# The expert stage in two phases, with the last four attention blocks routed inside the first

## The reference

```
probs = sigmoid(h @ router_w.T)                  # 8 experts
topw, sel = top_k(probs, 2); topw /= topw.sum(-1) + 1e-20
y = square(relu(h @ W1[e])) @ W2[e]              # widths 4 x 256, 4 x 512
out = x + gb * sum over the 2 chosen of topw * y
```

## Time and profile before

| | |
|---|---|
| median of 3 runs | 2789.18 us |
| profiled execution, first to last instruction | 2796.0 us |
| up to the end of attend | 2145.6 us |
| dispatch_rest and the start of experts, to the transposes of tile 1 | 112.0 us |
| from there to the last matmul of tile 38 | 470.0 us |
| last adds and gate_out | 68.4 us |

### The profile page before, as it was taken

One profiled execution on the slowest core, in us unless ns is written; L12 is line 12 of the kernel. 1 busy time (PEld: TensorE's weight loads), 2 busy tenths in 40 slices (PEclk: granted clock), 3 DMA queues, 4 the chain that ended last, 5 costly groups with the idle time before them and its releaser, 6 DMA issues. The chain is left out here.

```text
span 2796.0 us, 49392 instructions
## 1 busy us (share of the span) xinstructions
PE 2529.9 (90%) x16192; PEld 1298.9 (46%) x16192; DVE 2179.1 (78%) x5287; ACT 1727.6 (62%) x3481; POOL 692.7 (25%) x721
## 2 busy tenths in 40 slices
PE   7978999999999999999999999999996579999990
PEld 6852333333333333333333333333332479999990
DVE  6979889888888788888888898888821867777761
ACT  4640576777666666666666667666674257777760
POOL 3453333000010101011010110101012435556553
PEclk9986899999999999999999999999998689999995
DMA  6989788412404234040431404234012635555548
GB/s 213 316 280 301 275 282 286 145 27 57 97 28 97 56 73 116 13 117 29 96 92 37 120 22 104 52 78 105 16 54 84 217 84 92 88 90 91 91 68 255
DMA packets 218336, 331.82 MB, mean 119 GB/s; under 512 B 27408, under 2 KB 158224, under 8 KB 218096
## 3 DMA queue, kind: packets, MB, share of 16 engines
q1 hardware_dynamic: 137728, 170.48, 21.4%
q0 software_dynamic: 58704, 136.86, 19.7%
q10 hardware_dynamic: 21664, 21.50, 2.5%
HBM read 140.75 MB, written 187.20 MB: 117 GB/s over the span
## 5 line engine op out<-in xcount | busy, mean ns | idle before, releaser
L1007 ACT ACTIVATE probs<-ps 128x512 f32<-128x512 f32 (+3 forms) x2400 | 1122.2, 539 | 587.5 <-PE ps L1335 339.4
L1033 DVE TENSOR_REDUCE early<-ps 128x1 f32<-128x512 f32 x1536 | 1001.5, 684 | 106.0 <-PE ps L1240 100.1
L1240 PE MATMUL ps<-kh,qs 96*128 96x512 bf16 (+3 forms) x2560 | 882.2, 361 | 88.0 <-DVE early L1033 37.4
L1335 PE MATMUL ps<-qs,kh 99*128 99x512 bf16 (+3 forms) x2560 | 831.1, 352 | 17.0 <-ACT probs L1007 6.6
L1351 PE MATMUL ps<-probs,vs 128*32 128x512 f32 (+3 forms) x5120 | 605.8, 545 | 0.0
L1240 PEld LDWEIGHTS ps<-kh,qs 96*128 96x128 bf16 x2560 | 250.7, 99 | 700.5 <-DVE early L1033 303.6
L1029 DVE CUSTOM_DVE_ANT_0 junk<-ps,causal 128x128 bf16<-128x128 f32 (+3 forms) x1024 | 480.7, 483 | 52.8 <-PE ps L1240 48.0
L1335 PEld LDWEIGHTS ps<-qs,kh 99*128 99x128 bf16 x2560 | 246.1, 98 | 290.7 <-ACT probs L1007 135.8
L1760 POOL DMA_INDIRECT acc<-y,to x156 | 250.6, 1606 | 119.0 <-ACT y L1815 73.9
L926 POOL DMA_INDIRECT rows_out<-row,place_a x96 | 95.2, 991 | 698.5 <-DVE place_a L697 650.8
L1339 PE MATMUL ps<-ident_b,causal_b 128*128 128x128 bf16 x1024 | 214.0, 221 | 0.0
(11 more groups left out here) (231 smaller groups left out, 3011.2 us busy)
## 6 DMA issues: line engine op xcount, KB each, us to landing
rows_out<-row POOLq DMA_DIRECT2D x129, 544.0 KB, 3.6
xg<-rows_out SPq DMA_DIRECT2D x39, 544.0 KB
v_ones<-vt SPq DMA_DIRECT2D x16, 1024.0 KB, 6.4
vs<-v_ones SPq DMA_DIRECT2D x16, 1024.0 KB, 11.2
contexts<-ctx_out SPq DMA_DIRECT2D x64, 256.0 KB
q_parts<-parts SPq DMA_DIRECT2D x32, 384.0 KB, 4.6
k_parts<-parts SPq DMA_DIRECT2D x32, 384.0 KB, 4.6
qs<-q_parts SPq DMA_DIRECT2D x64, 192.0 KB, 7.3
```

The lines of the kernel that those rows point to most:

```text
L1007: nc.scalar.activation(probs[u % PB][:, h, q0:TB], bank(s % SB)[:, q0:TB], ACT.Exp, scale=SCALE).then_inc(exp_done, 1)
L1033: nc.vector.tensor_reduce(early[:, h, t, k0 // CW:k0 // CW + 1], tile, AX.X, ALU.max).then_inc(max_done, 1)
L1240: nc.tensor.matmul(tile[:, 0:w], qh[a % HR][0:STACK, t * P:(t + 1) * P], kh[a % HR][0:STACK, k0:k0 + w], start=True, stop=True).then_inc(m ...
L1335: mm = nc.tensor.matmul(tile[:, q0:TB], kh[a % HR][:, kt * P:(kt + 1) * P], qh[a % HR][:, j * TB + q0:(j + 1) * TB], start=True, stop=not ...
```

## The change

The table of tiles is made in two parts. After the 12 blocks of attend, at least FULL = 17 full tiles exist whatever the routing is. These are listed at once (`first_table`, 22 small DVE steps) and run first. The four late blocks are finished inside the steps of these tiles, at fixed steps: block m begins at step 1 + 12m, so one block takes part in three tiles. Then the table of the LATE = 22 tiles is made (`late_need`, `late_table`, `tile_rows` at steps 59 to 61), and these run as before. 17 + 22 is again 39. Other parts:

- w1 is loaded whole in attend (3.1 MB). w2 is loaded whole (3.1 MB) at the start of experts and split once into w2_hi and w2_lo: ACT makes four high parts of 1536 columns, DVE two low parts and POOL two; PE waits for all before its loop. The split per tile (L1797, L1872) is gone.
- Since w2 stays in place, `down` reads it at an address from a register, and PE computes that address by an instruction ahead of each of the 12 matmuls. Tiles of width 256 read a neighbour's slices, and relu's scale `wide` (0 or 1) zeroes the upper half.
- `down` adds up in the same two banks for every tile, and so waits in its first step for the `weigh` of the tile before. `tails` moves from POOL to DVE.
- The gate of attention is folded into wo_g once; square is in place.

```diff
+FULL = -(-(2 * HIDDEN_BLOCKS * TB - E * (TB - 1)) // TB)
+LATE = (2 * T - FULL * TB + E * (TB - 1)) // TB
+STEP_LAG = 2
+PITCH = 12
+BASE = [1 + PITCH * m for m in range(LATE_BLOCKS)]
+SECOND_TABLE = BASE[-1] + L_PUT + 1
+SEND_FROM = [(b + L_PUT + 1) // FW - 1 for b in BASE[:-1]] + [(BASE[-1] + L_PUT) // FW - 2]
+SENDS = [3] * (LATE_BLOCKS - 1) + [8]
...
+                def gather(i):
+                    if i == FULL:
+                        sp.wait_ge(table_steps, BOTH_TABLES)
+                        for p in range(2):
+                            sp.wait_ge(sent[p], 64 * LATE_BLOCKS)
...
+                for n in range(SPLITS // 2, SPLITS):
+                    own = slice(n * piece, (n + 1) * piece)
+                    pool.wait_ge(w2h_done, n + 1)
+                    nc.gpsimd.tensor_tensor(w2_lo[:, own, :], w2_lo[:, own, :].bitcast(F32),
+                                            w2_hi[:, own, :].bitcast(F32), ALU.subtract).then_inc(w2lp_done, 1)
...
+                def send(m, part):
+                    if part == 0:
+                        pool.wait_ge(placed, m + 1)
+                        pool.wait_ge(tails_set, 3 + m + 1)
...
+                for i in range(NT):
+                    add(i)
+                    for m in range(LATE_BLOCKS):
+                        done = SENDS[m] * (i - SEND_FROM[m])
+                        if 0 <= done < 2 * TT:
+                            for part in range(done, min(done + SENDS[m], 2 * TT)):
+                                send(m, part)
...
+                def tails(i):
+                    dve.reg_load(kind, tiles[0:1, i, 3:4])
+                    e = dve.snap(kind, min_val=0, max_val=E - 1)
+                    dve.wait_ge(xg_in[i % 2], 16 * (i // 2 + 1))
+                    if i >= 3:
+                        dve.wait_ge(y_done, TT * (i - 2))
+                        dve.wait_ge(added, 16 * TT * (i - 2))
...
                     if f == 1 and i + 1 < NT:
                         low_rows(i + 1)
+                        tails(i + 1)
+                    for m in range(LATE_BLOCKS):
+                        late(m, q - STEP_LAG - BASE[m])
+                    if q == SECOND_TABLE + STEP_LAG + 2:
+                        tile_rows(41, LATE, FULL)
...
                 def down(q):
                     i, f = divmod(q, FW)
-                    p = i % 2
+                    if f == 0:
+                        pe.reg_load(slab, tiles[0:1, i, 1:2])
+                        at["slice"] = pe.snap(slab, min_val=0, max_val=NW - FW)
                     pe.wait_ge(lo_done, q + 1)
                     for t in range(TT):
-                        o = bank(2 + 2 * p + t // 2)[:, (t % 2) * D:(t % 2 + 1) * D]
+                        if f == 0 and i and t % 2 == 0:
+                            pe.wait_ge(y_done, TT * (i - 1) + t + 2)
+                        o = bank(2 + t // 2)[:, (t % 2) * D:(t % 2 + 1) * D]
                         hi, lo = (h[q % HB][:, t * P:(t + 1) * P] for h in (hid_hi, hid_lo))
-                        nc.tensor.matmul(o, hi, w2_hi[p][:, f, :], start=(f == 0 and t % 2 == 0), stop=False,
-                                         skip_group_check=True)
+                        w_hi, w_lo = (w[:, bass.ds(at["slice"] + f, 1), :].squeeze(1) for w in (w2_hi, w2_lo))
+                        nc.tensor.matmul(o, hi, w_hi, start=(f == 0 and t % 2 == 0), stop=False, skip_group_check=True)
...
+                pe.wait_ge(w2l_done, SPLITS // 2)
+                pe.wait_ge(w2lp_done, SPLITS - SPLITS // 2)
                 for q in range(NQ):
...
```

More of the change, by code:

```diff
@@ new lines, in experts @@
+        h_lo = [sb(f"h_lo{p}", [P, KK, TB], F32R) for p in range(2)]
+        hid_hi = [sb(f"hid_hi{k}", [P, TB], F32R) for k in range(HB)]
+        hid_lo = [sb(f"hid_lo{k}", [P, TB], F32R) for k in range(HB)]
+        hid = [sb(f"hid{k}", [P, TB])[:, :] for k in range(HB)]
+        y = [sb(f"y{p}", [P, TT, D]) for p in range(2)]
+        span = max(FULL, LATE)
+        tiles = sb("tiles", [P, NT, 4], I32)
+        wide = sb("wide", [P, NT])
+        wo_g = sb("wo_g", [P, KK, D])
+        tile_i = sb("tile_i", [P, span], I32)
@@ new lines, in experts @@
+        tile_f = sb("tile_f", [P, span])
+        need_i = sb("need_i", [P, E], I32)
+        need = sb("need", [P, E])
+        ends = sb("ends", [P, E])
+        taken = sb("taken", [P, E])
+        shift = sb("shift", [P, E])
+        table = sb("table", [P, E, E])
+        past = sb("past", [P, span, E])
+        behind = sb("behind", [P, span, E])
+        which = sb("which", [P, span])
+        start = sb("start", [P, span])
+        source = sb("source", [P, span])
+        slices = sb("slices", [P, span])
@@ L1415, in dispatch_rest @@
         rstd = sb("rstd_r", [P, TT])
[L1416 to L1427, removed]
@@ L1495, in _ @@
-                pool.wait_ge(sent, 128 * len(blocks))
+                nc.gpsimd.iota(tile_i[:, :], [[1, span]], 0, 0).then_inc(tails_set, 1)
+                for p in range(2):
+                    nc.gpsimd.memset(row[p][:, :, D + E:ROW], 0.0).then_inc(tails_set, 1)
+                for n in range(SPLITS // 2, SPLITS):
[3 more added lines that the diff above has]
+                                            w2_hi[:, own, :].bitcast(F32), ALU.subtract).then_inc(w2lp_done, 1)
@@ new lines, in w2_high, with high_rows @@
+                def w2_high(n):
+                    own = slice(n * piece, (n + 1) * piece)
+                    if n == 0:
+                        act.wait_ge(raw_in, 16 * (1 + SPLITS))
+                    nc.scalar.activation(w2_hi[:, own, :], w2_lo[:, own, :].bitcast(F32), ACT.Copy).then_inc(w2h_done, 1)
+                def high_rows(i):
+                    for k in range(KK):
+                        act.wait_ge(g_mm, KK * i + k + 1)
+                        if i >= 2:
+                            act.wait_ge(u_mm, FW * (i - 1))
+                        nc.scalar.activation(h_hi[i % 2][:, k, :], bank(4 + k), ACT.Copy).then_inc(g_hi, 1)
@@ L1543, in residual @@
[L1543 to L1551 removed]
+                column, kind = dve.alloc_register("tile_column_d"), dve.alloc_register("tile_expert_d")
@@ new lines, in route, with count @@
+                def route(m):
+                    pe.wait_ge(h2t_done, KK * (m + 1))
+                    for t in range(TT):
+                        for k in range(KK):
+                            mm = nc.tensor.matmul(bank(6)[:, t * E:(t + 1) * E], h2t[:, k, t * P:(t + 1) * P],
+                                                  rw_s[:, k, :], start=(k == 0), stop=(k == KK - 1))
+                    mm.then_inc(r_mm, 1)
+                def count(m):
+                    pe.wait_ge(r_steps, RS * m + 8)
+                    pe.wait_ge(r_exp, m + 1)
+                    choice.count(nc, bank(6), keep).then_inc(count_mm, 1)
```

848 lines of the change are left out of this document (421 added, 427 removed).

## The result

| | before | after |
|---|---|---|
| median | 2788.58 us (4 runs) | 2774.11 us (4 runs, 2769.68 to 2776.39) |
| profiled execution, first to last instruction | 2796.0 us | 2774.3 us |
| up to the end of attend | 2145.6 | 2142.4 |
| from there to the transposes of tile 1 | 112.0 | 28.7 |
| from there to the transposes of tile 38 | 447.7 | 508.5 |

The ratio of the times is 0.9933, with a 95% interval from 0.9913 to 0.9952: 14.5 us less by the medians, against a forecast of 24. The two profiled executions differ by 21.7 us. The five stretches give it: -3.2 - 83.3 + 60.8 + 0.9 + 3.2 = -21.6.

What follows compares the result with a forecast made beforehand. PE was taken to bound the tiles, and a chain over all engines dispatch_rest, where PE waits about 107 us. Terms: -81.5 + 29 + 5 + 14 + 11.5 - 2 = -24 us, 2765 us; forecast 2753 to 2774, whole range 2745 to 2812.

Steps and rivals of the forecast that it cites:

- Start of the tiles: From the stage's start to tile 1's transposes: 112.0 us become 30.5, 81.5 us saved (77 to 86).
- The second slow start: In the start, PE's clock at 1.2 GHz again after its wait: up to 3.7 us, taken as 2.3.
- Late blocks on PE: Four late blocks' matmuls, transposes and counts among the tiles add to PE's time in full: 29 us (27 to 33).
- Count waits for ranks: PE's count in each late block waits for DVE's ranks, a little over 1 us late: 5 us for four (0 to 8).
- a sign of being wrong: In the late blocks: the forecast is wrong if DVE's late work stops PE in other places than the count.
- Addresses: In each tile's first `down`, address instructions at 0.14 us plus the output wait: 0.36 us per tile, 14 us (4 to 55).
- The two rivals built on a dearer issue: In `down`: 0.17 us per matmul, 2778 us, chance 0.18; or PE bound by its queue, up to 2806 us, slower, 0.21.
- That of 0.17 us: In `down`: a register-addressed matmul with its computation takes 0.17 us, 27 us instead of 14, 2778 us; chance 0.18.
- Join: Steps 61 to 64: sends, adds, tails and table make low part 61 late, stopping PE 11.1 us; 11.5 us in all (0 to 15).
- The rival in which the joins are absorbed: At join and counts: the steps' lead hides the 11.5 and 5 us, giving -40 us, 2749 us; chance 0.14.
- End: After the last matmul: weigh and tile 37's adds start earlier, so tile 38's add waits less: -2 us.
- w1 in attend: w1's load moved into attend costs nothing; up to 10 us if it delayed heads.

Runs made afterwards that it cites:

- e8_all: The edits of e1_count_later, e2_four_tails and e7_w2_halves together in the changed kernel; median 2748.1 us, ratio to before 0.9837.
- e9_three_sends: e8_all with only three of block 15's eight sends, so some rows never reach the experts (no candidate); 2743.3 us, one run.
- e10_sends_behind: e8_all with block 15's eight sends behind the adds of tile 13 instead of ahead of them; 2748.4 us, one run.
- e2_four_tails: Changed kernel with four buffers instead of three for share and to; median 2765.7 us, ratio to before 0.9906.
- e3_fixed_slice: Changed kernel with down reading fixed slices of w2's high parts, without register addresses and leaving work out (no candidate); median 2773.0 us, ratio to before 0.9925.
- e4_dve_low: Changed kernel with all four low parts of w2 made by DVE, none by POOL; median 2770.0 us, ratio to before 0.9912.
- e7_w2_halves: e4_dve_low with w2's first half split before tile 0's gathered rows arrive; median 2762.2 us, ratio to before 0.9889.
- e1_count_later: Changed kernel with each late block's count one step later in PE's list (L_COUNT 19 instead of 18); median 2762.8 us, ratio to before 0.9888.
- e11_between_adds: e8_all with block 15's eight sends in three pieces: three ahead of tile 13's adds, three behind their first, two behind their second; median 2747.0 us, ratio 0.9847.
- e12_four_and_four: e11_between_adds with block 15's eight sends in two pieces, four ahead of tile 13's adds, four behind their first; median 2746.3 us, ratio to before 0.9826.
- e5_fill: Changed kernel with twelve transposes of the identity on PE ahead of each count's wait, changing no result; median 2769.0 us, ratio to before 0.9919.

## Why the prediction was right, and where it was off

The mechanisms were the forecast ones: PE's idle stretch is gone, the late blocks cost PE their own time, and the join stops PE at the instruction that was named. The size was right in part by luck. The forecast of -24 us stands against -18.4 us for the stretches behind attend, and the medians gave -14.5, 2774.1 us, at the upper end of the forecast's 2753 to 2774. Term by term:

- **Start of the tiles.** 83.3 us saved, 81.5 forecast. The table took 5.5 us instead of 6.6, the gather 8.5 from table to transposes instead of 6.6 (so w2 beside it seems to have cost more than the 2 us I added; no run leaves w2 out), and POOL's end came at 28.6 us, 28.2 forecast. The second slow start fell behind tile 1's transposes, where it cost some 1.9 us (clock 0.87 over 14.3 us).
- **Late blocks on PE.** 29 us forecast. With no wait left, tiles 7 to 9 of e8_all, with one block's worth of work, take 16.67 + 13.96 + 13.24 = 43.9 us against 3 x 12.29: 7.0 us per block, 28. Right. (Tiles 1 to 15 of e8_all together, 212.5 us against 15 x 12.29 less the one `down` of 1.4 us that tile 1 lacks, give 29 for the four.)
- **Count waits for ranks.** 4.9 us, 5 forecast. But each of the last three made the clock fall, 1.6 us each; I had priced slow clock only behind the long idle time of the start. This is a missing term, 4.8 us. The prediction called it a sign of being wrong if DVE's late work stopped PE elsewhere than at the count; it did, for 0.6 us ahead of a block's transposes.
- **Addresses.** 0.15 us per tile, 6 us, where I took 0.36 and 14. The mechanism was right: in a tile's first `down` most matmuls start 0.12 to 0.13 us apart, with one address computation each, one or two in a tile 0.15 to 0.22, and the twelve take 1.57 us on average (tiles 18 to 37); in the other three steps the queue runs ahead and they take 1.41. Mis-sized were the distance (0.125 in the middle, 0.130 on average, not 0.14) and the wait for the outputs, which cost nothing. The start of one first `down`, its end, and the address computations:

```profile
2438.89 0.28 PE L1997 MATMUL ps<-w_hi,hid_hi 128*128 x1
2439.01 0.28 PE L1998 MATMUL ps<-w_lo,hid_hi 128*128 x1
2439.13 0.30 PE L1999 MATMUL ps<-w_hi,hid_lo 128*128 x1
...
2440.14 0.31 PE L1998 MATMUL ps<-w_lo,hid_hi 128*128 x1
2440.29 0.29 PE L1999 MATMUL ps<-w_hi,hid_lo 128*128 x1
2440.41 0.39 PE L1976 MATMUL ps<-h_hi,w_hi 128*128 128x512 f32 x1
...
L1997 PEldq FUSED_REGOPS  x624: 46/55/60, 2174.9 to 2702.0; - x156
```

  The two rivals built on a dearer issue are out. That of 0.17 us rested on rows in which half of the distance was no execution time; the average here is 0.130. The 62 ns per matmul in microcode of the Trainium skill (TensorE: Matmul & The Clock Gate, section "Step-by-step: what each phase is for") are not seen on top of that distance here either.
- **Join.** Idle 10.1 us where 11.1 was forecast, at the instruction that was named and by the chain that was named (adds, tails, table, low part 61). The slow clock behind it, 3.1 us, was again left out: 13.3 us in all against 11.5. The rival in which the joins are absorbed is out.
- **End.** -2 us forecast, +3.2 measured. The last adds did start earlier behind the last matmul (4.8 us, 6.5 in the earlier trace rows), but POOL's drain at the end of the stage takes 6.4 us instead of 3.3; the kernel before and the changed one:

```profile
L1724 POOLq DRAIN  x1: 3277/3277/3277, 2743.3 to 2743.3; - x1
...
L1491 POOLq DRAIN  x1: 6425/6425/6425, 2716.8 to 2716.8; - x1
```

  Before the change, dispatch_rest ended with a drain of its own of 2.7 us. With five sends fewer (e9_three_sends) it takes 6.2 us, but with all of them, only later, it takes 6.3 (e10_sends_behind). That it is the sends' part of the stage that makes it long fits 2.7 + 3.3 against 6.4; it was not tried by itself and stays open. Another 1.7 us came in gate_out, whose lines are unchanged (50.8 us against 49.1 from its first DMA to the end); no run says why.
- **w1 in attend.** At most 0.5 us: by so much the distance between the same matmuls of the two kernels changes across the load.

Of the 60.8 us between tiles 1 and 38, 28 are late work, 4.9 + 0.6 waits of the late blocks, 4.8 their slow clock, 13.3 the join, 5.6 addresses, 1.9 the slow start: 59.1, and 1.7 us are not accounted for. Too much for the addresses (8) and too little for clock and end (some 12) cancelled in part. Either error alone would have put the sum off by that much.

## What to carry to other kernels

Work that is moved from an idle stretch beside a bound engine costs its own time there; here a stretch of 112 us became 29, its work cost 28 us in the stage behind, and waits and slow clock at the seams took another 26. A move of one step, a fourth buffer and another order of the start gave 26 us back. Price each wait on TensorE twice, once for the idle time and once for the clock behind it; the second, 1.6 us here, comes in most executions and not in all, so two profiles can differ by one or two of them without any cause in the kernel. A stage's start is worth reading instruction by instruction: which split stands ahead of which arrival, and on which engine, was worth 7 us.

## What the runs showed of the hardware

- The granted clock fell to 0.50 for 3.4 us behind waits of about 1 us, but not behind all. The waits at the counts in the five kernels that have them (the changed kernel, e2_four_tails, e3_fixed_slice, e4_dve_low, e7_w2_halves):

  | PE's wait at the count, us | times | followed by the fall |
  |---|---|---|
  | 0.82 to 0.93 | 5 | 0 |
  | 1.04 to 1.18 | 10 | 8 |
  | 1.88 to 2.07 | 5 | 5 |

  In e1_count_later a wait of 1.28 us, ahead of a late block's transposes (2218.0), was not followed by it. So the length of the wait alone does not tell.
- Eight indirect DMAs in a row from POOL, 1.3 to 1.7 us apart, came with ACT idle while its inputs were there, for 4.7 us in e8_all and e2_four_tails and some 7 of 7.9 us in e10_sends_behind, and in the last two with gaps of 0.3 to 1.0 us between matmuls of PE that wait for nothing. This was so in eight executions of nine, not in that of the changed kernel; it was not so in the three executions with runs of two to four (e9_three_sends, e11_between_adds, e12_four_and_four). What is held up in between no row shows; it stays open.
- Attend, the same instructions each time, ended between 2134.4 and 2148.9 us in these executions. The mean granted clock of 175 to 2130 us differs between two of them, the first with tile 0's transposes at 2148.4 (e5_fill), the second at 2162.9 (e12_four_and_four):

```profile
175.00:2130.00 1955.00, 1839.46 (x12004) 689.18 (x12003) 1616.93 (x4263) 1268.56 (x2635) 287.01 (x369) 0.98 0.38 107
```

```profile
175.00:2130.00 1955.00, 1846.09 (x11909) 689.71 (x11907) 1618.48 (x4262) 1260.14 (x2624) 280.74 (x362) 0.97 0.38 106
```

  For an effect of 5 us in a later stage, the stretch of the trace tells more than a median of four runs. It is one execution all the same, and differences of 1 to 2 us between such stretches tell nothing.
